# Reciprocal roots on VectorE: a guess and two quadratics in 7 instructions, in place of a guess and three Newton steps in 11

## The chip, the cores and the metric

The kernel runs on one core of a Trainium2 chip. The metric is the device time of one execution in microseconds (us); lower is better.

## What is computed

The reference is a small vision model on 32 images of 3x96x96, in float32:

```python
h = leaky_relu(batchnorm(conv2d(x, stem_w, stem_b, 4)))          # 96 channels, 24x24
offset = conv2d(h, off_w, off_b, 4)                              # 32 channels, 6x6
h = leaky_relu(batchnorm(deform_conv(h, offset, dcn_w, dcn_b)))  # 36 tokens x 192
h = h + attn(_layernorm(h))    # linear attention, 12 heads, 64 features, projection,
                               # residual, then (y-mu)*rsqrt(var+eps)*gamma+beta
h = h + ffn(_layernorm(h))     # gate picks 1 of 3 experts, 192 -> 768 -> gelu -> 192
```

Batch norm takes `g / sqrt(v + eps)` for 3x96 channels once. Each token goes through three layer norms, so three times `1 / sqrt(var + eps)` is needed: ahead of the attention, at its end, and ahead of the experts.

## The kernel before, in words

The 32 images are worked in four groups (0 to 3) of 8 images, 288 tokens of 192 channels. A group's tokens lie in three row tiles (128, 128 and 32 tokens, `ROWTILES`). All engines run lists of instructions written by hand; nothing is scheduled by a program, and engines meet through counting semaphores. A function `step(g, ...)` per engine interleaves group g with the experts of group g-1 and, except in the last group, with the stem and the first gathers of group g+1.

The stages of a group, by what TensorE does:

- stem (L552, L574), transposes of the result into rows (L593) and the offset products (L604). VectorE turns the offsets into cell indices (`sample_points`, L1318 to L1341), and POOL gathers the cells (`gather`, indirect DMA issues on L519, nine batches of four). POOL also rearranges image rows for the stem (L474).
- corner sums and the deformable convolution, in nine turns: ScalarE makes the first product of a turn (L1074), VectorE adds three more (`combine`, L1356), TensorE transposes the sum (L656) and multiplies it (L668).
- the norm ahead of the attention: `norm_in` on VectorE. TensorE then transposes the result (L735) and ScalarE copies it out of the banks.
- attention (L750 to L838).
- `norms_out` on VectorE: the residual is added (L1470), the second norm follows (L1475, L1479), and directly behind it the third (L1392), whose three tiles TensorE transposes one by one (L735) and sums per image (L845). Behind that VectorE does the first turn of corner sums of the next group (L1356) and the last expert adds of the group before (L1532, L1547, and L1554 into `y_parts`).
- experts: L871 and L878 upwards, gelu on ScalarE (L1198), L899 and L903 downwards. TensorE does part of the previous group's expert work while VectorE is in `norms_out`. The second L871 of the next pass waits for `y_parts` (L1554).

Each norm begins with `moments`: `bn_stats` for the three tiles (L1382), `bn_aggr` (L1386), eps is added (L1388), and then `rsqrt` takes the root of the 128x3 variances (L1276 to L1281). `rsqrt` is used 13 times: once for the batch norms at the start (96x3), and three times in each group.

What orders the instructions inside such a piece is a `Chain`: each instruction adds one to a semaphore. `chain.add` does only that, `chain.link` also waits until the count is reached, so the next instruction starts when the result is written. The length of a chain is a constant (`RSQRT`, from which `MOMENTS` is made), and POOL's `pause` for its sixth batch (L494) waits for a count that is made from it, the end of the second norm's root.

Of the kernel before, what the change touches and what calls it, by code (L numbers as in the profile page):

```python
# [21 lines left out]
F32 = mybir.dt.float32  # L22
I32 = mybir.dt.int32
ALU = mybir.AluOpType
# [40 lines left out]
PART = C2 - WIDE  # L65
SLOPE = 0.01
EPS = 1e-5


def tables():  # L70
# [31 lines left out]
def build(nc, a, out):  # L102
# [6 lines left out]
    with ExitStack() as ctx:  # L109
# [147 lines left out]
        pool_turns, dve_turns = sem("pool_turns"), sem("dve_turns")  # L257

        IN_SBUF = 2
        RSQRT = 11  # L260
        MOMENTS = 7 + RSQRT

        def running(k):
# [1009 lines left out]
        def _(dve):  # L1273
            def rsqrt(chain, dst, x, ti, tt):

                chain.link(dve.tensor_scalar(ti.bitcast(I32) if ti.dtype != I32 else ti, x.bitcast(I32), 1, None, ALU.logical_shift_right))  # L1276
                chain.link(dve.tensor_scalar(dst.bitcast(I32), ti, -1.0, float(0x5F3759DF), ALU.mult, ALU.add))
                for _ in range(3):
                    chain.link(dve.tensor_tensor(tt, dst, dst, ALU.mult))
                    chain.link(dve.scalar_tensor_tensor(tt, tt, -0.5, x, ALU.mult, ALU.mult))  # L1280
                    chain.link(dve.scalar_tensor_tensor(dst, tt, 1.5, dst, ALU.add, ALU.mult))  # L1281


            def stem_xt(g, s=0):

# [93 lines left out]
            def moments(chain, src):  # L1379

                for t, (t0, n) in enumerate(ROWTILES):
                    chain.add(dve.bn_stats(stats[0:n, t, :], src[0:n, t, :]))  # L1382
                chain.wait()
                dve.sem_inc(dve_turns, 1)
                for t, (t0, n) in enumerate(ROWTILES):
                    chain.add(dve.bn_aggr(mvar[0:n, t, :], stats[0:n, t, :]))  # L1386
                chain.wait()
                chain.link(dve.tensor_scalar(rs_x[:, :], mvar[:, :, 1], EPS, None, ALU.add))  # L1388
                rsqrt(chain, rstd[:, :], rs_x[:, :], rs_i[:, :], rs_t[:, :])
# [175 lines left out]
            dve.tensor_copy(w_stem[:, :], ps[5][0:STEM_ROWS, 0:96]).then_inc(nat_evac, 1)  # L1565
            chain = Chain(dve, bn_chain, 0, 2 + RSQRT + 3)
            chain.link(dve.tensor_copy(bn[:, :, :], ps[5][0:96, 192:207]))
            chain.link(dve.tensor_scalar(bn_tmp[:, 0, :], bn[:, 4, :], EPS, None, ALU.add))
            rsqrt(chain, bn_scale[:, :], bn_tmp[:, 0, :], bn_tmp[:, 1, :].bitcast(I32), bn_bias[:, :])
            chain.link(dve.tensor_tensor(bn_scale[:, :], bn_scale[:, :], bn[:, 1, :], ALU.mult))  # L1570
            chain.link(dve.tensor_tensor(bn_bias[:, :], bn[:, 0, :], bn[:, 3, :], ALU.subtract))
# [128 lines left out]
```

How the kernel before makes its waits and increments, by code:

```python
            def wait(self, n=None):  # L338
                self.eng.wait_ge(self.s, self.g * self.per + (self.n if n is None else n))
# [18 lines left out]
            def load_images(g, s):  # L358
                second = (g, s) == (0, 1)
                if later(g):
                    sp.wait_ge(x_ready, 1 if (g, s) == (1, 0) else 2 * g + s)
                for b in range(SUB):
                    img = w["x"][bass.ds(g * GROUP + (SUB * s + b), 1)]
                    sp.dma_start((xs_second if second else xs)[GRID * b:GRID * (b + 1), :, :].rearrange("y (c k) x -> y c (k x)", c=CIN),
                                 img.rearrange("n c (y k) x -> (n y) c (k x)", k=STRIDE)).then_inc(x_second if second else x_in, 16)
# [1 line left out]
            def store_cells(g):  # L368
                if later(g):
                    for k in range(BATCHES - SLOTS, BATCHES):
                        sp.wait_ge(gathered[ring_slot(k)], slot_done(g - 1, k))
                for s in range(2):
                    sp.wait_ge(ht_even, 6 * g + 3 * (s + 1))
                    sp.wait_ge(ht_odd, 6 * g + 3 * (s + 1))
                    for slot in range(2):
                        first = PAD + s * SUB * GRID * GRID - slot * GRID
                        dst = table[first:first + ROWS * GRID, slot * C1:(slot + 1) * C1]
                        sp.dma_start(dst.rearrange("(p x) c -> p x c", p=ROWS), ht[:, s, :, :]).then_inc(h_stored[s], 16)
# [255 lines left out]
            def dcn_bias():  # L636
                pe.wait_ge(w_dcn_evac, 4)
                pe.wait_ge(ones_ready, 1)
```

## Time and profile before

| | us |
|---|---|
| median of 3 runs | 488.26 |
| lowest and highest run | 486.48, 488.51 |
| span of the profiled execution | 511.0 |

| engine | busy us (share of the span) |
|---|---|
| TensorE (PE) | 424.5 (83%) |
| VectorE (DVE) | 307.6 (60%) |
| ScalarE (ACT) | 227.5 (45%) |
| POOL | 159.0 (31%) |

The page gives the profiled execution no other time than its span, which is 22.7 us above the median of the runs. Rows of the timeline read: start, time from the first start to the last end of the merged instructions, engine, line of the kernel, operation, output <- inputs, shape, count, and in brackets the engine's idle time before them and what ended it. The mean granted clock of TensorE is 0.883 of full speed over the span.

### The profile page before, as it was taken

What the parts mean: (1) busy time and instruction counts of PE and PEld (TensorE: products, weight loads), DVE (VectorE), ACT (ScalarE), POOL (GpSimd) and SP (SyncE); (2) the same over time, 40 slices, a digit from 0 to 9 for tenths busy, and PEclk for the clock granted to TensorE, in tenths of its full rate; (3) what the DMA queues carried; (4) which work ended last, traced back from release to release, by engine and by line L of the source; (5) the groups of instructions that cost most, each with busy time, mean ns of one, the idle gap of its engine ahead of it and who ended that gap; (6) DMA issues with size and microseconds to landing.
All of it is one profiled execution on the core that took longest, in us unless ns stands there. A gap on an engine that the chain in (4) does not pass through costs nothing.

```text
span 511.0 us, 7813 instructions
## 1 busy us (share of the span) xinstructions
PE 424.5 (83%) x2630; PEld 298.8 (58%) x2630; DVE 307.6 (60%) x1180; ACT 227.5 (45%) x548; POOL 159.0 (31%) x168
## 2 busy tenths in 40 slices
PE   4992546599778989998798899799779888988997
PEld 2571333466474558665765685466647675666576
DVE  4561538453345778955369885844569895458222
ACT  2373335433435675344333753626245652652520
POOL 3106757201436552006265440005365410000000
PEclk9996669559985589999889999699799999999999
DMA  5559844659725332077234430086244310000000
GB/s 137 138 144 269 207 133 120 186 181 228 210 62 142 94 90 81 1 186 217 64 108 114 140 98 2 1 210 192 69 133 107 98 47 1 0 1 2 17 1 17
DMA packets 60022, 54.27 MB, mean 106 GB/s; under 512 B 44242, under 2 KB 52335, under 8 KB 59983
## 3 DMA queue, kind: packets, MB, share of 16 engines
q0 software_dynamic: 9216, 28.32, 19.6%
q1 hardware_dynamic: 50336, 25.42, 19.4%
q8 instruction: 21, 0.34, 0.3%
q14 instruction: 18, 0.15, 0.1%
q10 hardware_dynamic: 431, 0.03, 0.1%
HBM read 38.70 MB, written 15.06 MB: 105 GB/s over the span
## 4 chain that ended last, share of the span: by engine, by line
PE 64%; DVE 12%; ACT 8%; issue 6%; another core or an unknown queue 3%; POOL 3%; DMA 2%; ACTq 1%; DVEq 0%; POOLq 0%
PE bank L899 7%; PE bank L871 6%; PE bank L668 6%; PE bank L593 4%; PE bank L574 4%; PE bank L878 4%; PE bank L809 3%; PE bank L790 3%; PE bank L604 3%; POOL ring L519 3%; PE bank L794 2%; PE bank L825 2%; PE bank L750 2%; PE bank L552 2%
## 5 line engine op out<-in xcount | busy, mean ns | idle before, releaser
L519 POOL DMA_INDIRECT ring<-cells,cell x144 | 146.5, 1018 | 221.6 <-DVE cell L1334 100.0
L1356 DVE SCALAR_TENSOR_TENSOR bank<-ring,corner,bank 128x96 f32<-128x96 f32 x224 | 52.9, 312 | 26.1 <-ACT bank L1074 22.9
L668 PE MATMUL bank<-w_dcn,shared 128*128 128x192 f32 x192 | 44.8, 376 | 21.4 <-ACT shared L1083 13.2
L1198 ACT ACTIVATE hid<-bank,b_up 128x288 f32<-128x288 f32 x72 | 32.1, 497 | 63.6 <-PE bank L878 55.8
L871 PE MATMUL bank<-xfT,w_up 128*128 128x288 f32 x144 | 47.9, 458 | 5.8 <-ACT hid L1198 3.5
L668 PEld LDWEIGHTS bank<-w_dcn,shared 128*128 128x128 f32 x192 | 34.9, 212 | 30.3 <-ACT shared L1083 18.0
L899 PE MATMUL bank<-w_down,hid 128*128 128x192 f32 x288 | 52.1, 332 | 0.0
L899 PEld LDWEIGHTS bank<-w_down,hid 128*128 128x128 f32 x288 | 46.2, 190 | 4.6 <-issue 4.4
L871 PEld LDWEIGHTS bank<-xfT,w_up 128*128 128x128 f32 x144 | 27.0, 208 | 15.4 <-ACT hid L1198 5.7
L1074 ACT ACTIVATE bank<-ring,corner 128x96 f32<-128x96 f32 x112 | 31.4, 336 | 6.7 <-DMA ring<-cells,cell 5.5
L574 PE MATMUL bank<-xt,w_stem 48*96 48x384 f32 x96 | 32.6, 774 | 1.2 <-DVE h L1373 1.2
L1436 DVE COPY kv<-bank 64x153 f32<-64x153 f32 (+1 forms) x24 | 7.0, 291 | 41.4 <-PE bank L809 31.9
L1356 DVE SCALAR_TENSOR_TENSOR acc<-ring,corner,acc 128x96 f32<-128x96 f32 x96 | 22.7, 304 | 13.9 <-issue 11.1
L656 PE MATMUL bank<-ident_sb,acc 128*128 128x128 f32 x108 | 20.7, 307 | 12.1 <-issue 11.9
L593 PE MATMUL bank<-ident_sb,h 96*96 96x96 f32 x192 | 26.1, 294 | 3.3 <-ACT ring L1043 2.5
L1083 ACT ACTIVATE shared<-bank 128x384 f32<-128x384 f32 x36 | 17.4, 484 | 25.3 <-PE bank L656 20.3
L878 PE MATMUL bank<-xfT,w_up_rest 64*128 64x288 f32 x144 | 28.3, 470 | 0.0
L825 PE MATMUL bank<-kv,shared 128*108 128x102 f32 (+1 forms) x144 | 20.2, 302 | 9.5 <-DVE o L1449 9.1
L1356 DVE SCALAR_TENSOR_TENSOR acc<-ring,corner,bank 128x96 f32<-128x96 f32 x112 | 27.4, 303 | 0.0
L593 PEld LDWEIGHTS bank<-ident_sb,h 96*96 96x96 f32 x192 | 20.6, 151 | 10.9 <-issue 7.2
L1043 ACT ACTIVATE ring<-bank 96x384 f32<-96x384 f32 x36 | 16.6, 487 | 23.3 <-PE bank L593 23.3
L656 PEld LDWEIGHTS bank<-ident_sb,acc 128*128 128x128 f32 x108 | 14.7, 156 | 19.8 <-issue 18.7
(182 smaller groups left out, 699.0 us busy)
## 6 DMA issues: line engine op xcount, KB each, us to landing
cells<-ring SPq DMA_DIRECT2D x16, 864.0 KB, 8.1
xs<-in_x_dram SPq DMA_DIRECT2D x28, 108.0 KB
ring<-cells,cell POOLq DMA_INDIRECT x144
w_down<-in_L_ffn_W_dram SPq DMA_DIRECT2D x3, 576.0 KB, 7.1
hid<-in_L_tok_dcn_w_dram SPq DMA_DIRECT2D x1, 1152.0 KB, 7.6
w_up<-in_L_ffn_W_dram SPq DMA_DIRECT2D x3, 384.0 KB, 3.8
out_dram<-y SPq DMA_DIRECT2D x8, 96.0 KB, 2.2
w_up_rest<-in_L_ffn_W_dram SPq DMA_DIRECT2D x6, 96.0 KB, 4.2
```

The lines of the kernel that those rows point to most:

```text
L519: pool.indirect_dma_start(ring[:, ring_slot(k), j, :], None, table[0:HALF_CELLS, :] if k < EARLY else table, bass.IndirectOffsetOnAxis(ap= ...
L574: pe.matmul(stem_bank(g, n)[0:C1, 0:4 * ROWS], w_stem[at:at + STEM_K, :], xt[at:at + STEM_K, 4 * (i // 2):4 * (i // 2) + 4, :], start=True ...
L593: mm = pe.transpose(row_bank(g, u)[0:ROWS, C1 * i:C1 * (i + 1)], h[:, s, 4 * j + i, :], ident[0:C1, 0:C1])
L656: mm = pe.transpose(ps[2][:, 128 * i:128 * i + 128], acc[:, k % 3, i, :, :].rearrange("p j c -> p (j c)"), ident[:, :])
L668: mm = pe.matmul(tokens_out(t), samp[:, n % 2, i, :], w_dcn[:, CHUNKS * (k % QUADS) + i, :], start=(k % QUADS == 0 and i == 0), stop=(k % ...
L825: mm = pe.matmul(ps[2 + b][0:n, 102 * i:102 * i + 34 * ni], qp[:, p, t0:t0 + n], kv[:, t, p, 0:ni, :], start=True, stop=True)
L871: pe.matmul(up_bank(g, n)[:, 0:TOK], w_up[:, e, 128 * f:128 * f + 128], xfT[:, 0, :], start=True, stop=False)
L878: pe.matmul(up_bank(g, FCH * e + 2 * q + i)[:, 0:TOK], w_up_rest[lower(i), e, q, :], xfT[lower(i), 1, :], start=False, stop=True).then_inc ...
L899: mm = pe.matmul(down_out(e, t), hid[:, e % 2, f, t0:t0 + n], w_down[:, e, f, :], start=(f == 0), stop=(f == FCH - 1))
L1074: ins = act.activation(running(k)[:, :, j, :], ring[:, ring_slot(k), j, 0:C1].rearrange("p (i c) -> p i c", c=32), ACT.Copy, scale=corner[ ...
L1198: act.activation(hid[:, e % 2, f, :], up_bank(g, n)[:, 0:TOK], ACT.Gelu, bias=b_up[:, n:n + 1]).then_inc(gelu_done, 1)
L1356: ins = dve.scalar_tensor_tensor(acc[:, k % 3, :, j, :] if c == 3 else part_sum, ring[:, ring_slot(k), j, C1 * c:C1 * (c + 1)].rearrange(" ...
```

## The change

`rsqrt` is written anew. The guess is made in one instruction in place of two (the integer of x is multiplied by -0.5 and a constant added; the shift goes). The three Newton steps of three instructions each go. In their place the product t = s x y y is formed in two instructions, where y is the guess and s a scale, and a polynomial of fourth degree in t is evaluated as the product of two quadratics, in four instructions, the last two of which also multiply by the guess. The first quadratic is written to `q` with `chain.add`, so the instruction behind it has no wait on it. `x` is overwritten. `RSQRT` falls from 11 to 7.

```diff
+def root_factors():
+
+    lead = 0.27375925
+    scale = lead ** 0.25
+    factors = ((-0.90371225, 1.70764180), (-4.24306449, 5.26800198))
+    return scale, *((b * scale, c * scale * scale) for b, c in factors)
+
+
+ROOT = root_factors()
...
-        RSQRT = 11
+        RSQRT = 7
...
             def rsqrt(chain, dst, x, ti, tt):
 
-                chain.link(dve.tensor_scalar(ti.bitcast(I32) if ti.dtype != I32 else ti, x.bitcast(I32), 1, None, ALU.logical_shift_right))
-                chain.link(dve.tensor_scalar(dst.bitcast(I32), ti, -1.0, float(0x5F3759DF), ALU.mult, ALU.add))
-                for _ in range(3):
-                    chain.link(dve.tensor_tensor(tt, dst, dst, ALU.mult))
-                    chain.link(dve.scalar_tensor_tensor(tt, tt, -0.5, x, ALU.mult, ALU.mult))
-                    chain.link(dve.scalar_tensor_tensor(dst, tt, 1.5, dst, ALU.add, ALU.mult))
-
+                scale, (b1, c1), (b2, c2) = ROOT
+                q = ti.bitcast(F32)
+                chain.link(dve.tensor_scalar(dst.bitcast(I32), x.bitcast(I32), -0.5, float(0x5F376000), ALU.mult, ALU.add))
+                chain.link(dve.scalar_tensor_tensor(tt, x, scale, dst, ALU.mult, ALU.mult))
+                chain.link(dve.tensor_tensor(tt, tt, dst, ALU.mult))
+                chain.add(dve.scalar_tensor_tensor(q, tt, b1, tt, ALU.add, ALU.mult))
+                chain.link(dve.scalar_tensor_tensor(x, tt, b2, tt, ALU.add, ALU.mult))
+                chain.link(dve.scalar_tensor_tensor(x, x, c2, dst, ALU.add, ALU.mult))
+                chain.link(dve.scalar_tensor_tensor(dst, q, c1, x, ALU.add, ALU.mult))
```

VectorE's list in `norms_out` of group 1, from the first instruction of the third norm's root to the norm itself, before (`rs_x` is the variance with eps, `rs_i` the integer, `rs_t` the product, `rstd` the root):

```order
L1276 TENSOR_SCALAR rs_i<-rs_x 128x3
L1277 TENSOR_SCALAR rstd<-rs_i 128x3
L1279 TENSOR_TENSOR rs_t<-rstd 128x3
L1280 SCALAR_TENSOR_TENSOR rs_t<-rs_t,rs_x 128x3
L1281 SCALAR_TENSOR_TENSOR rstd<-rs_t,rstd 128x3
L1279 TENSOR_TENSOR rs_t<-rstd 128x3
L1280 SCALAR_TENSOR_TENSOR rs_t<-rs_t,rs_x 128x3
L1281 SCALAR_TENSOR_TENSOR rstd<-rs_t,rstd 128x3
L1279 TENSOR_TENSOR rs_t<-rstd 128x3
L1280 SCALAR_TENSOR_TENSOR rs_t<-rs_t,rs_x 128x3
L1281 SCALAR_TENSOR_TENSOR rstd<-rs_t,rstd 128x3
L1392 TENSOR_SCALAR shared<-h,mvar,rstd 128x192 x2
```

The three Newton steps are L1279 to L1281, three times. The same place with the change (the lines have moved by 13):

```order
L1289 TENSOR_SCALAR rstd<-rs_x 128x3
L1290 SCALAR_TENSOR_TENSOR rs_t<-rs_x,rstd 128x3
L1291 TENSOR_TENSOR rs_t<-rs_t,rstd 128x3
L1292 SCALAR_TENSOR_TENSOR rs_i<-rs_t 128x3
L1293 SCALAR_TENSOR_TENSOR rs_x<-rs_t 128x3
L1294 SCALAR_TENSOR_TENSOR rs_x<-rs_x,rstd 128x3
L1295 SCALAR_TENSOR_TENSOR rstd<-rs_i,rs_x 128x3
L1405 TENSOR_SCALAR shared<-h,mvar,rstd 128x192 x2
```

Eleven instructions have become seven; VectorE's whole list is 52 instructions shorter. The lists of TensorE, ScalarE, POOL and SP are the same as before.

## Rows read from the trace of the kernel before

**Rows 1.** Parts 1 and 4 of the page: TensorE's busy time, and the chain by engine

```profile
PE 424.5 (83%) x2630; PEld 298.8 (58%) x2630; DVE 307.6 (60%) x1180; ACT 227.5 (45%) x548; POOL 159.0 (31%) x168
...
PE 64%; DVE 12%; ACT 8%; issue 6%; another core or an unknown queue 3%; POOL 3%; DMA 2%; ACTq 1%; DVEq 0%; POOLq 0%
```

**Rows 2.** Timeline of VectorE, group 1 (start us, us, engine, line, operation, count, idle before)

```profile
264.20 0.17 DVE L1276 TENSOR_SCALAR rs_i<-rs_x 128x3 int32<-128x3 int32 x1
...
264.61 0.16 DVE L1279 TENSOR_TENSOR rs_t<-rstd 128x3 f32<-128x3 f32 x1
...
266.38 1.06 DVE L1475 SCALAR_TENSOR_TENSOR h<-xn,mvar,gamma_sb 128x192 f32<-128x192 f32 x3
```

**Rows 3.** Timeline of VectorE, two instructions without a wait between them

```profile
124.47 0.20 DVE L1332 SCALAR_TENSOR_TENSOR cell_f<-whole 128x36 f32<-128x36 f32 x1
...
124.58 0.23 DVE L1333 TENSOR_TENSOR hat<-pos,whole 128x72 f32<-128x72 f32 x1
```

**Rows 4.** VectorE's waits: timeline at the start, and the group of L1318

```profile
16.29 0.67 DVE L1298 TENSOR_SCALAR h<-bank,bn_scale,bn_bias 96x384 f32<-96x384 f32 x1 [2.31 <-PE bank L574]
...
L1318 DVE TENSOR_SCALAR part<-bank,offb_sb 128x288 f32<-128x288 f32 x4 | 2.1, 518 | 13.4 <-PE bank L604 13.4
```

**Rows 5.** Timelines of TensorE and VectorE, norm ahead of the attention, group 3

```profile
427.01 2.22 PE L899 MATMUL bank<-w_down,hid 128*128 128x192 f32 x12
...
428.00 0.95 DVE L1392 TENSOR_SCALAR xn<-h,mvar,rstd 128x192 f32<-128x192 f32 x3
```

**Rows 6.** Timelines of VectorE, POOL and TensorE, norms_out of group 0; a copy elsewhere

```profile
25.31 1.27 POOL L474 COPY xr<-xs 96x576 f32<-96x576 f32 x2 [4.15 <-issue]
...
164.94 2.29 DVE L1479 SCALAR_TENSOR_TENSOR h<-h,rstd 128x192 f32<-128x192 f32 x3
...
165.51 1.51 POOL L474 COPY xr<-xs 96x576 f32<-96x576 f32 x2
...
167.07 2.42 PE L552 MATMUL bank<-ident_sb,xr 96*112 96x96 f32 x12 [0.38 <-POOL xr L474]
...
171.39 1.16 DVE L1392 TENSOR_SCALAR shared<-h,mvar,rstd 128x192 f32<-128x192 f32 x3
...
173.97 1.41 PE L735 MATMUL bank<-ident_sb,shared 128*128 128x128 f32 x6
```

**Rows 7.** Timeline of TensorE, norms_out of group 1

```profile
269.70 0.84 PE L903 MATMUL bank<-w_down,hid 128*32 128x192 f32 x12 [1.66 <-issue]
...
272.73 1.05 PE L735 MATMUL bank<-ident_sb,shared 128*128 128x128 f32 x6
...
278.31 0.75 PE L871 MATMUL bank<-xfT,w_up 128*128 128x288 f32 x2 [0.49 <-DVE y_parts L1554]
```

**Rows 8.** Timeline of TensorE, norms_out of group 2

```profile
382.89 0.84 PE L903 MATMUL bank<-w_down,hid 128*32 128x192 f32 x12 [2.73 <-issue]
...
385.72 0.81 PE L735 MATMUL bank<-ident_sb,shared 128*128 128x128 f32 x6
...
389.83 1.37 PE L871 MATMUL bank<-xfT,w_up 128*128 128x288 f32 x4
```

**Rows 9.** Timeline of TensorE, norms_out of group 3

```profile
466.63 0.84 PE L903 MATMUL bank<-w_down,hid 128*32 128x192 f32 x12 [0.97 <-ACT hid L1198]
...
470.22 0.94 PE L735 MATMUL bank<-ident_sb,shared 128*128 128x128 f32 x6 [0.60 <-DVE shared L1392]
...
474.45 1.24 PE L871 MATMUL bank<-xfT,w_up 128*128 128x288 f32 x4
```

**Rows 10.** Timeline of POOL, gather issues of group 1

```profile
272.05 0.94 POOL L519 DMA_INDIRECT ring<-cells,cell  x1 [0.30 <-issue]
...
279.39 3.06 POOL L519 DMA_INDIRECT ring<-cells,cell  x1 [0.30 <-issue]
```

**Rows 11.** Granted clock: row of the windows view for one stretch; four L871 in group 0

```profile
160.00:182.00 22.00, 21.62 (x82) 12.63 (x81) 17.27 (x74) 13.47 (x25) 14.30 (x14) 0.50 0.32 91
...
177.62 2.29 PE L871 MATMUL bank<-xfT,w_up 128*128 128x288 f32 x4
```

## The prediction

> **What bounds the kernel now.** I read the page's parts 1 and 4 first: TensorE is busy 83% of the span and holds 64% of the chain that ended last, VectorE 12% [rows 1]. So most instructions taken from VectorE can only shorten time in which TensorE has something to do anyway. What counts is, at each of the 13 places where a reciprocal root is computed, whether TensorE waits for what follows the root. I therefore read VectorE's timeline for the price of a root, then TensorE's timeline around each place, and look for idle time put down to VectorE, or a group of matmuls stretched because its later operands came one by one.
>
> **Price of a root.** In group 1 the eleven linked instructions take from 264.20 to the next operation's start at 266.38, 2.18 us; the two integer ones take 0.41, so about 0.205 each, and the nine of the Newton steps 1.77, 0.197 each from start to start [rows 2]. All work on 128x3 elements, so what is paid is a fixed time per instruction, not arithmetic. The new form has one guess (0.205, priced as the old second integer instruction, of the same form), then six instructions. Five are waited for: 5 x 0.197 = 0.98. The sixth (the quadratic written to `q`) is added to the chain without a wait of its own. An unwaited pair shows what such a start costs: L1332 to L1333 starts 0.11 apart [rows 3]; the other bound is the linked 0.197. I take 0.11, the row of the same kind. New root: 0.205 + 0.98 + 0.11 = 1.30 us. **Saved per root: 0.88 us**; for the two roots of `norms_out`, 1.76; over 13 roots some 11.4 us of VectorE time. I now go through the places.
>
> **Start (batch-norm root), one place: 0.** Behind it VectorE applies the batch norm and still waits 2.31 us for stem matmuls L574 [rows 4]; those matmuls were never waiting for the root. The cover is the stem products themselves.
>
> **Norm ahead of the attention, groups 0 to 2: 0.** TensorE does the next group's row transposes and offset products at that time; the proof is on the other side: VectorE's next job for that group, L1318, waits for TensorE's L604 in all four occurrences, 13.4 us in sum [rows 4]. VectorE gains 0.88 and waits 0.88 longer.
>
> **The same norm in group 3: 0.** There is no next group. TensorE runs the last group's down product until 427.01 + 2.22 = 429.23; the three normalised tiles are there at 428.00 + 0.95 = 428.95 [rows 5]. If that cover went, up to 0.88 would be at stake here.
>
> **`norms_out`, group 0: 0 at the transposes, 0.24 ahead of them.** The last tile is ready at 171.39 + 1.16 = 172.55, while TensorE is in stem products until 173.97 [rows 6]. But in this stretch TensorE waited 0.38 us for POOL's rearranging copy L474, which took 1.51 beside VectorE's L1479; a copy of the same form elsewhere took 1.27, and the three L1479 took 2.29 [rows 6]. With the first root 0.88 shorter, L1479 is through before the copy starts, and L1382 (one tensor read) stands beside it. Bounds: 0 (the copy is as slow) and 0.38 (the wait goes whole); I take the copy's difference, 0.24. The Trainium skill (SBUF — State Buffer, "Who interferes with whom") says that a VectorE instruction with two SBUF inputs and a GpSimd one that reads SBUF exclude each other for the whole instruction, and that one with a single input, outside the two-port modes, does not. By that rule the copy would be at its 1.27 and the sum below 1.83; if any VectorE work held it up alike the sum would be 1.59.
>
> **`norms_out`, group 1: 0.73.** The transposes L735 take 1.05 against 0.81 for the same six in group 2, so 0.24 is waiting for tiles; and L871's second half waits 0.49 for `y_parts` L1554 [rows 7], which VectorE reaches only after both roots, the norm, a turn of corner sums and the expert adds. Both waits are within the 1.76 saved, so both go: 0.24 + 0.49 = 0.73. Next late is TensorE itself.
>
> **`norms_out`, group 2: 0.13.** No wait at L735 (0.81); L871 takes 1.37 against 1.24 in group 3 [rows 8, 9]. The cover is a gap of 2.73 us at L903, a wait that hangs on ScalarE's gelu and not on VectorE [rows 8].
>
> **`norms_out`, group 3: 0.73.** L735 waits 0.60 for the norm L1392, and takes 0.94 against 0.81, 0.13 more [rows 8, 9]. After it everything to the end is a chain of TensorE, so it arrives in full.
>
> **Moved beside it.** In groups 0 to 2 the first corner sums L1356 now start some 1.8 us earlier and meet POOL's last gather issue of its fifth batch. In group 1 such an issue takes 0.94, and the one that meets the later corner sums 3.06 [rows 10]. So one gather may come 2.1 us later, which I cost at nothing: by the code ScalarE reads that slot in the fourth turn of corner sums, and only the first is running. The next batch, released by those sums, starts earlier. No queue has other work: the order on TensorE, ScalarE, POOL and SP is unchanged, and POOL's pause on the chain counts the shorter chain.
>
> **Sum:** 0.24 + 0.73 + 0.13 + 0.73 = 1.83 us of 11.4. The profiled execution's span is 511.0 us, 22.7 above the median of 488.26; I take the difference over as it is, since the terms are waits and not shares: 488.26 - 1.83 = 486.4, -0.4%.
>
> **Rivals.**
> - *More comes through.* The covers in groups 1 and 2 contain gaps of 1.66 and 2.73 us at L903, where group 3 has 0.97 [rows 7, 8, 9]: 0.69 and 1.76 us that may belong to this one execution, whose span is 22.7 us over the median. Without them group 1 gives 0.73 + 0.69 = 1.42, and group 2 0.13 + 1.76 = 1.89, capped at the 1.76 saved. Sum 0.24 + 1.42 + 1.76 + 0.73 = 4.15, so 484.1. For: the excess must lie somewhere. Against: both groups that have gathers beside them show a long gap, so it may belong to the kernel and not to the execution. Chance 0.33.
> - *Little or nothing arrives.* The new instructions cost more than thought (the guess now multiplies an integer by a fraction, which no row shows), or the waits of 0.1 to 0.6 us are not those of an ordinary run. At 0.28 for each new instruction a root saves 0.2 and the sum is about 0.2 + 0.2 + 0.1 + 0.4 = 0.9, and the floor is 0: 487.4 to 488.3. This holds also the case that the change does not do what it says. Chance 0.13.
> - *Slower: TensorE's clock.* In 160 to 182 us, the same stage of group 0, the granted clock was 0.50, the 1.2 GHz level, and four L871 took 2.29 us; in group 3, at 1.00, they took 1.24 [rows 9, 11], 1.85 times less. If the shifted work made the clock stay low in this stage of group 1 or 2, each us of TensorE work there would cost 0.85 more: 2.2 us of work cancel the gain, 5.0 make the kernel 0.5% slower, and 8 us would cost 6.8, giving 488.26 - 1.83 + 6.8 = 493.2. Against: the change shortens idle time of TensorE and adds none. The Trainium skill (TensorE: Matmul & The Clock Gate, Part 1) says that activity releases the throttle, and that how much runs at the lower rate differs between runs of one kernel; by the first the clock could only gain, by the second some risk stays. Chance 0.07.
>
> **Numbers.** The forecast, 486.4, has chance 0.47; its own range is 485.6 to 487.3, from the bounds of its terms and the spread of the three runs. Over 0.5% is about what a measurement of this kernel can tell from no change; it is 2.4 us, so 485.8. Faster by more: the whole first rival and 0.06 of the forecast, 0.39. Slower by more: most of the clock's case, 0.06. Within: the rest, 0.55. The range reaches to the first rival's 484.1 with 0.3 for spread, 483.8, and up to no gain at all, 488.3; outside remain the slow case and the edges, under 0.2.
>
> **What would show it.** In the new profile: a root at 1.30 us from first start to the next operation, twelve times, with 0.11 behind the unwaited instruction; VectorE's busy time down by some 8.5 us (52 instructions of 0.16 to 0.17); L1318's waits for L604 longer, not shorter; POOL's copy of group 0 at 1.27; no wait for `y_parts` in group 1; L735 at 0.81 with no wait in group 3; and the gaps at L903 in groups 1 and 2 either as they were (forecast) or near 0.97 (first rival). I am wrong if roots are not near 1.30, if the granted clock of the stages of groups 1 to 3 changes, or if TensorE's stages behind the other norms shorten as well.

## The result, and the profile after

| | before | with the change |
|---|---|---|
| median, us | 488.57 (20 runs, 485.61 to 495.41) | 486.59 (20 runs, 481.45 to 490.14) |
| ratio, 95% interval | | 0.9956 (0.9934 to 0.9977) |
| span of the profiled execution, us | 511.0 | 485.7 |
| mean granted clock in it | 0.883 | 0.908 |

The kernel is 0.44% faster, 2.15 us, with an interval of 1.1 to 3.2 us. The two spans say something else: 25 us less. They can't be compared, and why not is the first finding below. The ratios here leave out the executions that ran in a slower state (of the first repeat of the kernel before only 3 of 12 count, and single runs on that chip took up to 909 us), while the medians are of all executions, so a ratio is not the quotient of the two medians beside it. In the kernel after, all lines have moved by 11 or 13 (L871 is L882, L903 is L914, L735 is L746, L1318 is L1331; the root is L1289 to L1295).

Parts 1 and 4 of the page after, which answer to [rows 1]:

```profile
PE 412.6 (85%) x2630; PEld 290.0 (60%) x2630; DVE 295.8 (61%) x1128; ACT 227.6 (47%) x548; POOL 156.2 (32%) x168
...
PE 64%; DVE 11%; ACT 9%; POOL 6%; issue 6%; DMA 3%; ACTq 1%; DVEq 0%; POOLq 0%
```

VectorE has 52 instructions and 11.8 us less to do. TensorE's 11.9 us less are no work of its own: it has the same 2630 matmuls, at another clock. The entry "another core or an unknown queue 3%", which stood in the chain before, is gone.

The root in VectorE's timeline after, group 0, as [rows 2] had it:

```profile
148.74 0.17 DVE L1289 TENSOR_SCALAR rstd<-rs_x 128x3 int32<-128x3 int32 x1
...
149.34 0.16 DVE L1292 SCALAR_TENSOR_TENSOR rs_i<-rs_t 128x3 f32<-128x3 f32 x1
149.42 0.15 DVE L1293 SCALAR_TENSOR_TENSOR rs_x<-rs_t 128x3 f32<-128x3 f32 x1
149.61 0.16 DVE L1294 SCALAR_TENSOR_TENSOR rs_x<-rs_x,rstd 128x3 f32<-128x3 f32 x1
...
150.00 1.13 DVE L1488 SCALAR_TENSOR_TENSOR h<-xn,mvar,gamma_sb 128x192 f32<-128x192 f32 x3
```

From 148.74 to 150.00 it is 1.26 us, against 2.18 before. From start to start the linked instructions cost 0.19 to 0.20 each, and the unwaited L1293 starts 0.08 behind L1292. The guess with its multiplication by a fraction costs 0.21 (the instruction behind it starts at 148.95).

TensorE's timeline after in the same places as [rows 7 to 9], groups 1, 2 and 3 from above:

```profile
250.39 0.84 PE L914 MATMUL bank<-w_down,hid 128*32 128x192 f32 x12 [0.97 <-ACT hid L1209]
...
253.22 0.81 PE L746 MATMUL bank<-ident_sb,shared 128*128 128x128 f32 x6
...
257.33 1.33 PE L882 MATMUL bank<-xfT,w_up 128*128 128x288 f32 x4
...
358.54 0.84 PE L914 MATMUL bank<-w_down,hid 128*32 128x192 f32 x12 [0.98 <-ACT hid L1209]
...
361.37 0.81 PE L746 MATMUL bank<-ident_sb,shared 128*128 128x128 f32 x6
...
442.24 0.84 PE L914 MATMUL bank<-w_down,hid 128*32 128x192 f32 x12 [0.97 <-ACT hid L1209]
...
445.07 0.81 PE L746 MATMUL bank<-ident_sb,shared 128*128 128x128 f32 x6
```

The transposes L746 wait for nothing and take 0.81 three times; the wait for `y_parts` is gone. And the gaps ahead of L914, which had been 1.66 and 2.73 us in groups 1 and 2, are 0.97 and 0.98 like group 3's. The waits of VectorE for the offset products, 13.4 us in [rows 4], in its group of VectorE lines, grew:

```profile
L1331 DVE TENSOR_SCALAR part<-bank,offb_sb 128x288 f32<-128x288 f32 x4 | 2.1, 518 | 15.9 <-PE bank L615 15.9
```

In group 0 POOL's copy took 1.37 (1.51 before), VectorE's L1492 (L1479 before) 1.48 in place of 2.29, and the matmuls behind the copy [rows 6] no longer wait:

```profile
151.06 1.48 DVE L1492 SCALAR_TENSOR_TENSOR h<-h,rstd 128x192 f32<-128x192 f32 x3
```

```profile
152.30 1.37 POOL L485 COPY xr<-xs 96x576 f32<-96x576 f32 x2
```

```profile
153.73 2.42 PE L563 MATMUL bank<-ident_sb,xr 96*112 96x96 f32 x12
```

### The profile page after: what moved, and what is told of

It is laid out like the page before. It is cut to its first block, busy times and chain, and to the rows that moved or that the text cites. A ratio compares the mean times of both kernels' runs of the same rounds, so it can differ in the third digit from the quotient of the medians.

```text
span 485.7 us, 7761 instructions
## 1 busy us (share of the span) xinstructions
PE 412.6 (85%) x2630; PEld 290.0 (60%) x2630; DVE 295.8 (61%) x1128; ACT 227.6 (47%) x548; POOL 156.2 (32%) x168
## 4 chain that ended last, share of the span: by engine, by line
PE 64%; DVE 11%; ACT 9%; POOL 6%; issue 6%; DMA 3%; ACTq 1%; DVEq 0%; POOLq 0%
PE bank L910 9%; PE bank L882 7%; POOL ring L530 6%; PE bank L604 5%; PE bank L889 4%; PE bank L585 4%; PE bank L679 4%; PE bank L615 4%; PE bank L801 3%; PE bank L820 3%; PE bank L805 2%; PE bank L761 2%; PE bank L563 2%; DMA ring<-cells,cell 2%; DVE o L1462 2%
## 5 line engine op out<-in xcount | busy, mean ns | idle before, releaser
L530 POOL DMA_INDIRECT ring<-cells,cell x144 | 143.8, 998 | 202.7 <-DVE cell L1347 67.9
L679 PE MATMUL bank<-w_dcn,shared 128*128 128x192 f32 x192 | 42.3, 360 | 15.4 <-ACT shared L1094 15.4
L882 PE MATMUL bank<-xfT,w_up 128*128 128x288 f32 x144 | 44.5, 433 | 5.5 <-ACT hid L1209 5.3
L679 PEld LDWEIGHTS bank<-w_dcn,shared 128*128 128x128 f32 x192 | 33.2, 202 | 24.0 <-ACT shared L1094 20.1
L882 PEld LDWEIGHTS bank<-xfT,w_up 128*128 128x128 f32 x144 | 25.0, 193 | 14.4 <-ACT hid L1209 7.8
L667 PE MATMUL bank<-ident_sb,acc 128*128 128x128 f32 x108 | 19.5, 292 | 15.0 <-issue 13.6
L604 PE MATMUL bank<-ident_sb,h 96*96 96x96 f32 x192 | 27.1, 300 | 3.1 <-ACT ring L1054 1.9
L667 PEld LDWEIGHTS bank<-ident_sb,acc 128*128 128x128 f32 x108 | 13.7, 148 | 22.6 <-issue 19.8
L1046 ACT ACTIVATE h<-bank,bn_bias,bn_scale 96x384 f32<-96x384 f32 x30 | 18.7, 662 | 15.7 <-PE bank L585 15.5
```

Of the source, the lines that this page charges most:

```text
L530: pool.indirect_dma_start(ring[:, ring_slot(k), j, :], None, table[0:HALF_CELLS, :] if k < EARLY else table, bass.IndirectOffsetOnAxis(ap= ...
L604: mm = pe.transpose(row_bank(g, u)[0:ROWS, C1 * i:C1 * (i + 1)], h[:, s, 4 * j + i, :], ident[0:C1, 0:C1])
L667: mm = pe.transpose(ps[2][:, 128 * i:128 * i + 128], acc[:, k % 3, i, :, :].rearrange("p j c -> p (j c)"), ident[:, :])
L679: mm = pe.matmul(tokens_out(t), samp[:, n % 2, i, :], w_dcn[:, CHUNKS * (k % QUADS) + i, :], start=(k % QUADS == 0 and i == 0), stop=(k % ...
L882: pe.matmul(up_bank(g, n)[:, 0:TOK], w_up[:, e, 128 * f:128 * f + 128], xfT[:, 0, :], start=True, stop=False)
```

## The experiments

Theory: the gain is time in which TensorE waited in and just behind `norms_out`, and nothing else. Rivals: a part comes from the other roots; nothing reaches the end, and the 0.44% is chance. Open as well is whether the two long gaps are a property of the kernel. Seven kernels ran in twelve measurements, in three batches, each batch on one chip. On the chips of the first and third batch the kernel before took 514.11 and 514.83 us, on that of the second 489.67.

The measure used throughout, beside the time, is the distance on TensorE between matmuls with the same place in its list, which is the same 2630 in all kernels: from the first projection product (L834 before) to the first sum per image (L845), the stage in which `norms_out` lies. All these numbers are differences of matmul starts.

**1. The kernel before, once more, twice.** No edit.

> The kernel before, unchanged, for a second profile of it (the first had a span of 511.0 us, 22.7 above the median) and for the floor of the comparison. My theory (the terms of the sum are the kernel's own waits): ratio 1.000; span near 487; in norms_out of group 3 TensorE waits 0.60 us for the norm again; the gaps of TensorE ahead of L903 in groups 1 and 2 stay at 1.66 and 2.73 us, with 0.24 and 0 us of waiting at L735. Rival (more was covered by accident): both gaps are near 0.97 us, as in group 3, and L735 in groups 1 and 2 waits for VectorE about 0.8 us each, with more than 1 us in all up to the second L871.

514.08 us, ratio 0.9936 (0.9878 to 0.9993) to the identical kernel before: so on this chip an interval can miss 1 by a little without any cause, and a difference of 0.5% can't be read there. The span was 511.7 and not near 487. The gaps ahead of L903 were 1.43 and 1.60 in groups 1 and 2: long again, but not of the sizes that the theory named. The second L871 waited for `y_parts` in both groups, 0.48 and 0.49.

> The kernel before, unchanged, once more, for a profile in which ScalarE is not held up in the attention of groups 0 to 2. Between the first projection matmul and the first image sum TensorE took 19.66, 15.86, 16.49 and 15.63 us in groups 0 to 3 in the first profile, and 18.67, 14.74, 14.73 and 14.73 in the changed kernel's. My theory (terms are the kernel's own waits): 15.6 to 15.9 in groups 1 to 3 and 19.3 to 19.7 in group 0, and 0.5 us more of waiting for y_parts in groups 1 and 2; ratio 1.000. Rival (these stages have the changed kernel's length in an undisturbed run, and the gain lies elsewhere): 14.7 to 15.0 in groups 1 and 2.

488.30 us, ratio 0.9986 (0.9957 to 1.0015), span 491.3. TensorE's timeline of this execution, groups 1 and 2, shows the waits without the long gaps:

```profile
248.47 0.84 PE L903 MATMUL bank<-w_down,hid 128*32 128x192 f32 x12 [0.97 <-ACT hid L1198]
...
252.18 1.06 PE L735 MATMUL bank<-ident_sb,shared 128*128 128x128 f32 x6 [0.72 <-DVE shared L1392]
...
257.78 0.75 PE L871 MATMUL bank<-xfT,w_up 128*128 128x288 f32 x2 [0.49 <-DVE y_parts L1554]
...
365.29 0.93 PE L735 MATMUL bank<-ident_sb,shared 128*128 128x128 f32 x6 [0.86 <-DVE shared L1392]
...
370.77 0.75 PE L871 MATMUL bank<-xfT,w_up 128*128 128x288 f32 x2 [0.49 <-DVE y_parts L1554]
```

Groups 1 and 2 are alike: a wait for the normalised tiles and one for `y_parts` in each. That is not what [rows 7, 8] showed, where group 1 had the second and a part of the first, and group 2 neither. ScalarE explains it. Its waits with no named source, first in the profile that the prediction was made from, the three largest at a named tile:

```profile
ACT hid L1198 <- issue: 6.8, 3, 4.3
ACT h L1062 <- remote: 6.3, 3, 3.5
ACT shared L1083 <- remote: 5.0, 2, 3.6
```

(sum, count, longest, in us). In the second repeat and in the profile after no such wait stands at these lines; in the first repeat they stand again (L1083 6.5 us, L1198 5.4). So the execution of 511.0 us has the length and the waits of the chips of batches 1 and 3, and what the prediction took for a cover in groups 1 and 2 was ScalarE's gelu held up there.

**2. The whole change**, on the faster chip beside the kernel before. The instructions are those of the change.

> The whole change again, written with a root of its own for each use (the instructions are the same). My theory: ratio near 0.9956, the four stages at 18.7, 14.7, 14.7 and 14.7 us. Rival (the measured 0.44% is chance): ratio within 0.2% of 1.

486.61 us, ratio 0.9941 (0.9907 to 0.9974), the same as the first measurement, 0.9956. So the gain is no chance. The stage in groups 0 to 3, us:

| kernel | g0 | g1 | g2 | g3 |
|---|---|---|---|---|
| before (profile of the prediction, slower chip) | 19.66 | 15.86 | 16.49 | 15.63 |
| before, repeat | 19.29 | 15.87 | 15.88 | 15.63 |
| with the change | 18.67 | 14.73 | 14.73 | 14.73 |
| the whole change, again | 19.34 | 14.73 | 14.73 | 14.73 |
| root with one quadratic | 18.50 | 14.74 | 14.74 | 14.74 |

(The last row is experiment 7 on the faster chip; g0 to g3 are the groups.) From the repeat of the kernel before the change takes off 1.14, 1.15 and 0.90 in groups 1 to 3. Group 0's stage runs at a granted clock of 0.50 to 0.52, and how much of it runs above 0.50 differs: 19.34 was not the 18.7 expected. Where both kernels had 0.50 throughout, it is 19.66 before and 19.34 with the new root. Behind the stage the wait for `y_parts` is worth 0.65 from start to start, in groups 1 and 2 (0.49 as idle time: the modelled end of the matmul before it lies past the point where the next could have begun).

**3. The new root in `norms_out` only.** `rsqrt` is given per place:

```diff
-            def moments(chain, src):
+            def moments(chain, src, rsqrt):
...
-                moments(chain, h2)
+                moments(chain, h2, rsqrt_in)
...
-                moments(chain, xn)
+                moments(chain, xn, rsqrt_out)
...
-                moments(chain, h3)
+                moments(chain, h3, rsqrt_out)
```

`rsqrt_in` (and the root at the start) is the old function of 11 instructions, `rsqrt_out` the new one of 7, and `MOMENTS` is counted apart for each.

> The new root in norms_out alone (8 of 13 places); the start and the norm ahead of the attention keep the Newton steps. My theory: the whole gain comes from here, ratio 0.9956 as for the whole change, about -1.8 to -2.2 us. Rival (the gain is spread over all places, since 4 of 13 roots' instructions are also shorter elsewhere): 8/13 of it, ratio 0.9973.

> New root only for the two norms at the end of the attention; the start and the norm ahead of the attention keep the Newton steps. Theory (all of the gain is waits of TensorE in and behind norms_out): TensorE's distance from the first projection product to the first sum per image is 14.73 us in groups 1 to 3, as with the whole change (15.88, 15.88 and 15.63 in the repeat of the kernel before); no wait for y_parts L1554's place; ratio to before 0.990 to 0.997, like the whole change's 0.9941. Rival (a part comes from VectorE being free earlier at the start and ahead of the attention): some of these distances stay above 15, or the ratio lies at 0.998 or above.

512.58 us, ratio 1.0002 (0.9964 to 1.0040), and 511.94, 1.0005 (0.9954 to 1.0056); both on chips of the slower kind. By the time alone the theory would fall: both ratios lie outside what it asked for (0.9956, then 0.990 to 0.997). The traces tell more. Group 3's stage, which has no gathers beside it, is 14.73 both times, the whole 0.90. In groups 1 and 2 it is 18.14 and 15.75, then 15.75 and 18.52, and not the 14.73 expected. In the second of them, TensorE ahead of the down products of group 2, and ScalarE at the same place:

```profile
380.56 0.84 PE L915 MATMUL bank<-w_down,hid 128*32 128x192 f32 x12 [3.08 <-ACT hid L1210]
381.33 3.17 PE L911 MATMUL bank<-w_down,hid 128*128 128x192 f32 x9
```

```profile
378.58 0.50 ACT L1210 ACTIVATE hid<-bank,b_up 128x288 f32<-128x288 f32 x1 [3.99 <-PE bank L890]
380.01 0.50 ACT L1210 ACTIVATE hid<-bank,b_up 128x288 f32<-128x288 f32 x1 [0.92 <-remote]
```

Two gelus that run back to back elsewhere (x2 in 0.89) start 1.43 apart, the gap at the down products is 3.08 and not 0.97, and nine of the matmuls behind it take 3.17 us, where twelve take 2.22 at full clock.

This is not the new root's doing. The same gap and the stage in all executions on the slower chips, the prediction's profile counted among them, in us (* marks a stage whose granted clock was 0.79 to 0.91 in the mean; it was 1.00 in all others):

| kernel | gap g1 | stage g1 | gap g2 | stage g2 |
|---|---|---|---|---|
| before (profile of the prediction) | 1.66 | 15.86 | 2.73 | 16.49 |
| before, first repeat | 1.43 | 15.87 | 1.60 | 16.19 |
| new root elsewhere only (experiment 4) | 7.49 | 22.93* | 1.45 | 15.90 |
| the same, again | 1.43 | 15.87 | 3.42 | 18.81* |
| new root in `norms_out` only | 2.70 | 18.14* | 2.12 | 15.75 |
| the same, again | 1.99 | 15.75 | 3.08 | 18.52* |
| quadratic linked too (experiment 6) | 0.98 | 14.72 | 1.39 | 15.01 |
| one quadratic (experiment 7) | 2.69 | 16.45 | 1.45 | 15.05 |
| longer root (experiment 5) | 2.73 | 17.95 | 7.63 | 23.88* |

With the new root in `norms_out` and the clock at 1.00, the stage is 14.73 plus what the gap has above 0.97, to within 0.16. With the old root gaps up to 1.66 leave it at 15.86 to 16.19, because the tiles of the norm come last there, and 2.73 makes it 16.49, which is 14.73 + 1.76. So a long gap hides a part of the gain, and one of 2.73 all of it in this stage; and the stretches at the lower clock come with either root.

**4. The new root everywhere but in `norms_out`.**

> The new root at the start and ahead of the attention (5 of 13 places); norms_out keeps the Newton steps. My theory: all five are covered by TensorE, 0.0 us, ratio 1.000 (0.998 to 1.002), and VectorE's waits for the offset products grow by what the roots save. Rival (spread over all places): 5/13 of the gain, ratio 0.9983; or more, if group 3's norm, covered by 0.3 us only, has less cover in ordinary runs.

> The reverse: new root only at the start and in the norm ahead of the attention, Newton steps in norms_out. Theory: the distances from projection to first sum per image are as before (15.9, 15.9, 15.6 in groups 1 to 3), the y_parts waits of 0.5 us stay, the waits of the cell offsets for TensorE's offset products grow, and the ratio is 0.998 to 1.002. Rival: 0.997 or less, and stages ahead of the attention are shorter.

516.77 us, ratio 0.9983 (0.9933 to 1.0032), and 514.64, 1.0013 (0.9968 to 1.0059). Nothing that these intervals can tell from 0; the first lies on the rival's 0.9983 and holds the theory's 1.000 as well. TensorE in group 3 of the second, against the same place of the kernel with the root in `norms_out` only:

```profile
473.58 0.93 PE L747 MATMUL bank<-ident_sb,shared 128*128 128x128 f32 x6 [0.61 <-DVE shared L1428]
```

```profile
468.67 0.81 PE L747 MATMUL bank<-ident_sb,shared 128*128 128x128 f32 x6
```

The stage of group 3 is 15.62 and 15.63 here, 14.73 there. From the last product of group 3's deformable convolution to its first attention product, the stretch with the norm ahead of the attention, it is 8.25 us in every kernel of this study, also where that norm has the old root. Group 1's stretch with that norm, from its first L681 to its first attention product (L750), is 12.72 to 12.75 in all of them. In groups 0 and 2 it varies between executions by more than a root saves, and so does TensorE's first stretch, up to the first transposes of corner sums (16.02 to 16.74 us, in no order by the root). So the roots outside `norms_out` give nothing where the distances can tell, and the two inside give all of the gain that is found.

**5. A longer root in `norms_out`**, the old one with a fourth Newton step (14 instructions), Newton roots elsewhere.

```diff
-                for _ in range(3):
+                for _ in range(4):
```

> A fourth Newton step in norms_out alone: three linked instructions more per root, 0.59 us, 1.18 per norms_out; everything else as before. My theory: what is exposed goes through in full: 1.18 us in group 3 and in group 1, 1.0 in group 2 (0.13 of it exposed already, so nearly all), 0 in group 0, together +2.4 to +3.5 us, ratio 1.005 to 1.007. Rival (the exposed waits are small accidents, and slack covers the rest): under +1 us, ratio below 1.002.

> A fourth Newton step in norms_out alone once more (+0.59 us a root, +1.18 per norms_out). My theory: group 3's stage becomes 16.8 us (15.63 + 1.18), as do those of groups 1 and 2, group 0's stays within 0.4 of 19.7; in all +3.5 to +4.5 us, ratio 1.007 to 1.009. Rival (slack covers most): under +1 us. On the other chip it was 1.0144 (1.0088 to 1.0200), more than the work added can explain if it is exposed once per root; if 1.014 comes back, something besides the roots' length is at work.

519.37 us, ratio 1.0144 (1.0088 to 1.0200), and on the faster chip 495.11, 1.0117 (1.0049 to 1.0185). Two roots are 6 x 0.197 = 1.18 us longer. From the waits of TensorE (sum, count, longest), the repeat of before and this kernel on the same chip:

```profile
PE bank L735 <- DVE shared L1392: 2.2, 3, 0.9
```

```profile
PE bank L747 <- DVE shared L1422: 5.6, 3, 1.9
```

3.4 us more in three groups, nearly 3 x 1.18. In distances the stages of groups 1 and 2 grew from 15.87 and 15.88 to 16.87, 1.0 each, so most of what was added comes through. And group 3's stage grew by 2.96, not 1.18:

```profile
449.03 0.93 PE L747 MATMUL bank<-ident_sb,shared 128*128 128x128 f32 x6 [1.88 <-DVE shared L1422]
449.90 3.90 PE L911 MATMUL bank<-w_down,hid 128*128 128x192 f32 x12
```

```profile
440.00:450.00 10.00, 7.14 (x49) 5.16 (x47) 8.72 (x44) 1.20 (x3) 0.00 (x0) 1.00 0.00 0
450.00:460.00 10.00, 10.00 (x49) 7.69 (x50) 3.39 (x12) 2.72 (x7) 0.00 (x0) 0.83 0.08 24
```

(rows of the windows view: busy time of TensorE, its loads, VectorE, ScalarE and POOL, then the granted clock). The twelve L911 behind the wait take 3.90 us against 2.22: behind 10 us with TensorE busy for 7.14 the granted clock fell to 0.83 in the mean of the next ten. The wait costs 1.27 here and the clock 1.68. But the longer wait is not enough for that. The first execution of the same kernel, at the same place:

```profile
480.60 0.93 PE L747 MATMUL bank<-ident_sb,shared 128*128 128x128 f32 x6 [1.88 <-DVE shared L1422]
481.46 2.22 PE L911 MATMUL bank<-w_down,hid 128*128 128x192 f32 x12
```

```profile
480.60:490.60 10.00, 10.00 (x60) 6.94 (x60) 4.24 (x15) 2.88 (x7) 0.00 (x0) 1.00 0.08 24
470.60:480.60 10.00, 7.14 (x49) 5.25 (x45) 8.60 (x46) 1.78 (x4) 0.00 (x0) 1.00 0.00 1
```

The wait is again 1.88, the ten us before it (second row) have again 7.14 of TensorE's work, and behind it (first row) the clock stays at 1.00; the stage is 16.90, 1.27 more than before. Of four waits of 1.84 to 1.88 here one was followed by the lower clock. Both ratios are above what the theory asked for (1.005 to 1.007, then 1.007 to 1.009), though the second's interval reaches down to it. In the second profile the waits and the clock of group 3 add up to 5.1 us, about the 5.7 us that its ratio says.

**6. The quadratic linked too**, so that nothing in the root goes unwaited.

```diff
-                chain.add(dve.scalar_tensor_tensor(q, tt, b1, tt, ALU.add, ALU.mult))
+                chain.link(dve.scalar_tensor_tensor(q, tt, b1, tt, ALU.add, ALU.mult))
```

> The change with the first quadratic linked too, so that the instruction behind it waits like the others. This prices the missing wait: a root takes 1.35 to 1.38 us from its first start to the next operation's, against 1.26 with the change, if an instruction behind a waited one starts 0.197 after it and behind an unwaited one 0.08 to 0.11. In time nothing: both roots of norms_out together would be 0.2 us longer and stay within what the 1.8 us saved leaves over, so the stages from projection to first sum per image stay at 14.73 in groups 1 to 3. Rival (the roots still set these stages): 14.9 or more.

509.82 us, ratio 0.9908 (0.9855 to 0.9960), on the third chip. VectorE's timeline in group 3:

```profile
457.17 0.17 DVE L1314 TENSOR_SCALAR rstd<-rs_x 128x3 int32<-128x3 int32 x1
...
457.77 0.16 DVE L1317 SCALAR_TENSOR_TENSOR rs_i<-rs_t 128x3 f32<-128x3 f32 x1
457.96 0.16 DVE L1318 SCALAR_TENSOR_TENSOR rs_x<-rs_t 128x3 f32<-128x3 f32 x1
...
458.55 1.06 DVE L1514 SCALAR_TENSOR_TENSOR h<-xn,mvar,gamma_sb 128x192 f32<-128x192 f32 x3
```

1.38 us per root, and 0.19 from L1317 to L1318 where the change has 0.08: the missing wait is worth 0.12 us a root. In the stages it is worth nothing: those of groups 1 and 3 are 14.72 and 14.74, and group 2's 15.01 has its excess in the gap ahead of the down products (1.39), as in experiment 3. Behind the stage a little of it shows: from the first sum per image to the first gate product (L852 before) group 1 takes 3.40 us, where the change has 3.26, so `y_parts` is still a little late there. That the ratio is lower than the whole change's on the other chip isn't explained; on a chip where the kernel before differs from itself by 0.6% it needs no explanation.

**7. A shorter root**: one quadratic in place of two, 5 instructions, all linked. The result is coarser.

```diff
+ONE = (0.6126131489955803, -2.0431927488887784, 1.876392330436907)
...
                 chain.link(dve.tensor_scalar(dst.bitcast(I32), x.bitcast(I32), -0.5, float(0x5F376000), ALU.mult, ALU.add))
+                chain.link(dve.scalar_tensor_tensor(tt, x, ONE[0], dst, ALU.mult, ALU.mult))
+                chain.link(dve.tensor_tensor(tt, tt, dst, ALU.mult))
+                chain.link(dve.scalar_tensor_tensor(tt, tt, ONE[1], tt, ALU.add, ALU.mult))
+                chain.link(dve.scalar_tensor_tensor(dst, tt, ONE[2], dst, ALU.add, ALU.mult))
```

> A root in 5 instructions at all 13 places: the same guess and one quadratic in place of two, all linked, with coefficients fitted for the one (the root's relative error is 2.5e-5 by the fit). A root should take 0.205 + 4 x 0.197 = 0.99 us, 0.31 less than with two quadratics. My theory: TensorE is now next late behind norms_out in all groups (L735 takes 0.81 us without a wait in the changed kernel), so nothing more comes: ratio the same as the whole change's, 0.9956, within 0.1%. Rival (VectorE still sets these stages' ends): another 3 x 0.62 = 1.9 us, ratio 0.992.

> Repeat of the root with one quadratic (5 instructions) beside the others on one chip. If the norms no longer hold TensorE up once the 7-instruction form is in, the stages from projection to first sum per image are again 14.73 us in groups 1 to 3, and its ratio differs from the whole change's 0.9941 by no more than its interval. If a shorter root still gives something, these stages are below 14.6, or the ratio is again near 0.992.

485.94 us, ratio 0.9922 (0.9888 to 0.9957), and on the third chip 509.41, 0.9959 (0.9915 to 1.0003). The root takes 0.99 us, and on the faster chip the stages are 14.74 as with seven instructions; on the third chip they are 16.45, 15.05 and 14.73, longer by the gaps in the table of experiment 3. So the waits at the norms were used up by the change already. Behind them 0.1 us more goes in groups 1 and 2 (3.17 from the first sum per image to the first gate product, against 3.26 and 3.27). The first ratio is the rival's 0.992 and not the 0.9956 of the theory, but the repeat is 0.9959 and the stages speak against the rival; the lower median (0.7 us under the whole change, on the same chip) is within the intervals of both. It is the fastest of the kernels that ran, but not shown to be faster than the change.

## Why the prediction was right, and where it was not

The predicted 486.4 us stands against 486.59, the range holds it, and the likeliest of the three classes (within 0.5%) came. The sum behind it was less good than its result.

- **Price of a root**: 1.30 predicted, 1.26 measured; saved 0.92, not 0.88. The unwaited start was 0.08, not 0.11. VectorE's busy time fell by 11.8, not 8.5; the overlap of the unwaited pair was left out (0.08 in each root, 1 us in all), and L1492 beside POOL's copy fell from 2.29 to 1.48. The rest of the difference was not followed up.
- **Start, and the norm ahead of the attention: 0.** Right for the norm in groups 1 and 3, by the 12.72 to 12.75 and the 8.25 us of every kernel, and VectorE's waits at L1331 grew as foretold. For the start and groups 0 and 2 nothing speaks against it, but no distance is fine enough to show it.
- **Group 0: 0.24.** TensorE's wait for the copy, 0.38, went whole (0.32 from start to start, by the 19.66 and 19.34 of the stage at the lower clock). The copy took 1.37, between the 1.27 of the SBUF rule and the 1.51 of no effect: when it started at 152.30, L1492 was ending and one-tensor reads stood beside most of it. So the Trainium skill's rule (SBUF — State Buffer, "Who interferes with whom") is right in direction here, and L1492 itself is where it shows, 2.29 to 1.48. The root with one quadratic shows it whole: the two-input reads (L1507 there) are through before the copy starts, only one-input reads stand beside it, and it takes 1.27:

```profile
149.18 1.06 DVE L1507 SCALAR_TENSOR_TENSOR h<-h,rstd 128x192 f32<-128x192 f32 x3
150.27 0.87 DVE L1410 BATCH_NORM_STATS2 stats<-h 128x6 f32<-128x192 f32 x3
```

```profile
150.74 1.27 POOL L487 COPY xr<-xs 96x576 f32<-96x576 f32 x2
```

- **Group 1: 0.73.** Measured 1.14 in the stage and 0.65 behind it, 1.79.
- **Group 2: 0.13.** This is the step that failed: "The cover is a gap of 2.73 us at L903". Measured 1.15 and 0.65, 1.80. In the profiled execution the gap was a cover indeed (16.49 is 14.73 + 1.76, so the change would have gained nothing in that stage). But it was ScalarE held up in an execution like those on the slower chips, and "I take the difference over as it is" carried it to executions that don't have it. There the norms are the last to arrive, and the two roots' 1.84 come through almost whole, in both groups. The first rival had the gaps right, with 1.42 and 1.76; its 1.42 was still 0.4 short.
- **Group 3: 0.73.** Measured 0.90. The mechanism is right; the wait read as 0.60 of idle time is 0.78 from start to start (0.90 less the 0.12 to 0.13 of the stretched L735).
- **Moved beside it.** POOL's last gather issue of the fifth batch took 1.07 us in group 1 and 1.08 in group 2, beside the corner sums, and not 3.06; the gather that might have come 2.1 us later didn't.
- **Sum of waits removed**: 0.32 + 1.79 + 1.80 + 0.90 = 4.8 us on the faster chip, against 1.83 in the forecast and 4.15 in the rival. The time fell by 2.15 (1.1 to 3.2), and in the second comparison, ratio 0.9941, by 2.9 us (1.3 to 4.6). The interval of the first excludes both 4.15 and 4.8, that of the second only 4.8. By the first, at least 1.6 us of what the waits gave went elsewhere, and the forecast came out because two errors met, too few waits and no loss behind them: its number was luck, its terms for groups 0 and 3 and for the price of a root were not.

**Where the rest went is only partly known.** What differs between executions of one kernel, matmul by matmul, are single stretches at the lower clock. The repeat of before had one at 268 us (six L668 in 2.29 us against 1.24) that the profile after had not; the whole change, run again, needed 72.94 us from group 0's sums per image to group 1's kv products, against 71.34 in both of these. On the second chip the kernel before had 489.50 us and a mean granted clock of 0.9097 in the mean of 41 runs, with a spread (standard deviation) of 2.2 us, and time and clock go together (correlation -0.76, -244 us per 1.0 of clock). The whole change had 0.9065 (12 runs), the first measurement's 20 runs 0.9049, the shorter root 0.9082. By that slope 0.0032 is 0.8 us and 0.0048 is 1.2 us given back, so that at equal clock the change would be worth some 3.3 to 3.7 us (2.15 + 1.2 and 2.9 + 0.8). That is an estimate from a slope. The difference in clock is little more than its uncertainty (0.0025 for 12 runs), the 0.0048 compares two measurements, the changed kernel's own slope is flatter (-168 in 12 runs, -176 in 20), and no run changed the clock alone. The prediction's slow rival asked for 8 us of work at the lower rate; of its mechanism a smaller dose may be there. The rule that it weighed (the Trainium skill, TensorE: Matmul & The Clock Gate, Part 1: activity releases the throttle, and the part run at the lower rate differs between runs) is borne out in its second half by these spreads. For its first half little speaks: in experiment 5 one of four longer waits was followed by the lower clock, and the whole change, with less waiting, did not show a higher mean.

Not tried: the two halves of the change on a chip of the faster kind, where the time might have settled what here only the distances on TensorE show.

## What to carry to other kernels

A gap on the bounding engine covers a late operand only if it is there in the executions that are timed: compare the same place in groups that should be alike, and where the profiled span is far above the median, get a second profile before a gap is used as a cover. Small linked instructions are paid by the piece (here 0.197 us each for 128x3 elements), and it pays to count them only between the last operand of a stage and the engine that waits for it: of 13 roots the 8 in `norms_out` mattered, those of group 0 by 0.3 us only. Once the waits are gone, a still shorter root brings next to nothing. So measure distances between instructions as well as times; a change of 0.4% can be seen in them long before the medians separate.

## What the runs showed of the hardware that was not expected

- **Chips differ**, or their state at the time does, since each was used in one batch only. The same kernel before took 488.57 and 489.67 us in two measurements and 514.11 and 514.83 on two other chips, 5% more. On these ScalarE is held up by as much as 9.6 us at a time (waits marked "issue" or "remote") in groups 0 to 2, which have gathers; from the first product with `kv` to the first of the projection it is 10.55, 11.58 and 11.68 us in groups 0 to 2 of the prediction's profile against 7.78, 7.96 and 7.82 on the faster chip, and in group 3, without gathers, 7.82 on both. What holds it up, no run shows.
- **A VectorE instruction without a wait** starts 0.08 us behind one on 128x3 elements, one with a wait 0.19 to 0.20; with the wait put back (experiment 6) the root takes 1.38 us in place of 1.26.
- **A wait may cost twice, or not.** In one execution 1.27 us more of waiting in group 3 were followed by 1.68 us lost at the lower clock. In another of the same kernel the same wait, behind as much work, was followed by none, and so were the waits of 0.6 to 0.9 in the repeat of the kernel before. What decides it, these runs don't show.
- **A copy and two-input reads.** In the kernel with the longer root, where the copy of group 0 falls on VectorE's L1505, three of these take 2.54 us against 1.06 elsewhere, and the copy its 1.27; in the kernel before, both were longer (2.29 and 1.51).
